# Latent-attention layer on one core: GpSimd forms the keys' rotary products from a copy made by ScalarE, zeros run on TensorE at the front, weight parts are shared out

## The reference, cut to what matters

```
xn  = layernorm(x)                                   # x [1, 2048, 512]
q   = xn @ wq                -> 16 heads of 128 + 64 (rotary part)
kva = xn @ wkv_a             -> ckv [2048, 128], k_pe [2048, 64]
ckv = ckv * rsqrt(mean(ckv^2) + eps) * kv_norm_scale
k_nope, v = ckv @ wkv_b      # per head 128 + 128
q_pe, k_pe = rope(q_pe), rope(k_pe)                  # k_pe is shared by all heads
attn = softmax(causal((q . k) * 192^-0.5)) ; out = (attn @ v) @ wo
x + out + (sum_r xn @ factors[r]) / sqrt(8) + bias
rope: [x1 * cos - x2 * sin, x2 * cos + x1 * sin]     # x1, x2: halves of 32
```

## Time and profile before

| | |
|---|---|
| median of 3 runs | 1505.07 us (1504.54 to 1505.99) |
| profiled execution, its own time | 1505.5 us |
| its span | 1503.7 us |
| busy: PE, DVE, ACT, POOL | 98%, 67%, 64%, 61% of the span |
| the span's first slice of 37.6 us | PE 50%, POOL 30% |
| first exponential of unit 0 starts | 61.43 us |

### The profile page before, as it was taken

The page is one execution under the profiler, slowest core; times in us unless marked ns, Lnnn a source line. Parts: engine busy times, 40 slices in busy tenths (PEclk is TensorE's granted clock), DMA queues, the critical chain, the costliest instruction groups (busy, mean ns, idle before and its releaser), DMA issues.

```text
span 1503.7 us, 25751 instructions
## 1 busy us (share of the span) xinstructions
PE 1471.3 (98%) x7908; PEld 755.5 (50%) x7908; DVE 1012.9 (67%) x2563; ACT 966.3 (64%) x2404; POOL 912.3 (61%) x919
## 2 busy tenths in 40 slices
PE   5999999999999999999999999999999999999997
PEld 5544555454545545445444444445555555455553
DVE  7877677777777766655555565566656666676776
ACT  7877767686866567566466666665546656654554
POOL 3688777675665456575465666656546555664553
PEclk9999999999999999999999999999999999999999
DMA  6599999987776597787577677886856677754554
GB/s 202 153 206 206 204 190 186 180 172 152 155 158 128 122 202 146 140 176 138 117 150 140 138 133 148 176 147 137 152 115 135 143 132 150 158 134 96 118 124 105
DMA packets 646615, 227.84 MB, mean 152 GB/s; under 512 B 599376, under 2 KB 612176, under 8 KB 646096
## 3 DMA queue, kind: packets, MB, share of 16 engines
q1 hardware_dynamic: 646480, 226.20, 73.6%
HBM read 65.67 MB, written 17.83 MB: 56 GB/s over the span
## 4 chain that ended last, share of the span: by engine, by line
PE 82%; ACT 6%; DVE 5%; issue 3%; POOL 3%; DMA 1%; SPq 0%; ACTq 0%; DVEq 0%; POOLq 0%
PE ps L423 17%; PE ps L424 16%; PE ps L425 16%; PE ps L574 6%; PE ps L579 6%; PE ps L580 6%; PE ps L576 6%; PE ps L575 6%; ACT ex L809 4%; POOL st L1400 2%; DVE gm L1166 1%; DVE ps L1168 1%; DMA acc<-x_in 0%; POOL q L1384 0%; ACT sqr L730 0%
## 5 line engine op out<-in xcount | busy, mean ns | idle before, releaser
L1400 POOL TENSOR_TENSOR st<-ex,st 128x512 f16<-128x512 f32 (+3 forms) x640 | 637.6, 1016 | 492.1 <-ACT st L819 482.2
L809 ACT ACTIVATE ex<-ps,nm,scales 128x512 f32<-128x512 f32 (+3 forms) x640 | 452.4, 709 | 459.0 <-DVE nm L1185 443.4
L1166 DVE TENSOR_REDUCE gm<-ps 128x1 f32<-128x512 f32 (+1 forms) x384 | 248.9, 668 | 168.8 <-PE ps L580 164.6
L819 ACT ACTIVATE st<-ex 128x512 f16<-128x512 f32 (+3 forms) x640 | 341.3, 561 | 6.1 <-ACT ex L809 0.4
L574 PE MATMUL ps<-kTh,q 128*128 128x512 f16 (+3 forms) x640 | 222.3, 347 | 6.8 <-ACT ex L809 4.5
L579 PE MATMUL ps<-kRh,q 128*128 128x512 f16 (+3 forms) x640 | 222.2, 347 | 2.5 <-POOL q L1384 2.5
L423 PE MATMUL ps<-pT,vH 128*128 128x512 f16 (+3 forms) x640 | 222.1, 347 | 0.6 <-DMA pT<-st 0.6
L580 PE MATMUL ps<-kRl,q 128*128 128x512 f16 (+3 forms) x640 | 222.1, 347 | 0.0
L575 PE MATMUL ps<-kTl,q 128*128 128x512 f16 (+3 forms) x640 | 222.1, 347 | 0.0
L576 PE MATMUL ps<-kTh,q 128*128 128x512 f16 (+3 forms) x640 | 222.1, 347 | 0.0
L424 PE MATMUL ps<-pT,vH 128*128 128x512 f16 (+3 forms) x640 | 222.1, 347 | 0.0
(11 more groups left out here) (202 smaller groups left out, 2141.3 us busy)
## 6 DMA issues: line engine op xcount, KB each, us to landing
wA<-w_abs SPq DMA_DIRECT2D x48, 256.0 KB, 2.9
wV<-w_vo SPq DMA_DIRECT2D x48, 256.0 KB, 2.9
pT<-st SPq DMA_TRANSPOSE x640, 3.3
fland<-factors_in SPq DMA_DIRECT2D x28, 256.0 KB, 3.0
wP<-w_pe SPq DMA_DIRECT2D x24, 256.0 KB, 3.0
wsq<-wq_in SPq DMA_DIRECT2D x16, 256.0 KB, 3.8
wso<-wo_in SPq DMA_DIRECT2D x16, 256.0 KB, 3.0
w_abs<-wA SPq DMA_DIRECT2D x16, 256.0 KB, 2.1
```

What stands on the lines that cost most here:

```text
L809: e.activation(ex[:, n % NEX, 0:keys], s_bank(n)[:, 0:keys], ACT.Exp, bias=nm[:, (i * QT + r) % 4:(i * QT + r) % 4 + 1], scale=scales[:, p ...
L819: e.activation(stage(n, keys)[:, :, 0, :], ex[:, n % NEX, 0:keys].rearrange("p (t n) -> p t n", n=P), ACT.Copy).then_inc(z["a_pH"], 1)
L1166: e.tensor_reduce(m, b, AX_X, ALU.max).then_inc(z["v_max"], 1)
L1400: e.tensor_tensor(s[:, :, 1, :], ex[:, n % NEX, 0:keys].rearrange("p (t n) -> p t n", n=P), s[:, :, 0, :], ALU.subtract).then_inc(z["g_pL" ...
```

## The change

1. The rotary products of the keys move from VectorE to GpSimd. GpSimd cannot take them from where TensorE left them, so ScalarE first copies the 64 raw numbers of both tiles into a new buffer `raw` (one instruction for a pair). VectorE keeps only the reciprocal, and its semaphore `v_kva` now stands for that.
2. The last tile (15) is normalized by GpSimd instead of ScalarE.
3. TensorE multiplies zeros (columns of the mask that are 0) before the first transposes (11 matmuls of 384 columns), before the norm of `wa` (5) and before the first latent product (7).
4. The low part of `wa` is halved: VectorE makes k blocks 0 and 1, GpSimd blocks 2 and 3 in two steps; TensorE waits for the second half between block 1 and block 2. VectorE makes it, and tile 1's low part, ahead of the statistics of pair 2; ScalarE makes tile 1's high part ahead of `wa`.
5. ScalarE makes the high parts of `wX` and `wA` for head 0, which VectorE made.
6. Squares of weights stand at other steps on ScalarE (`sq1` at step 1, `sqk` at 2, `sq0` at 3), and GpSimd normalizes tile 3 before it scales the key weights.
7. Two pairs of semaphores are merged (`v_rd` into `v_ts`, `d_bias2` into `d_bias`), which leaves the same instructions and the same waits.

```diff
-GTILES = tuple(range(3, 14, 2))
+GTILES = tuple(range(3, 16, 2))
...
@@ TensorE
+                    if t == 0 and k4 == KE // 2:
+                        e.wait_ge(z["g_wa"], 2)
...
+            def keep_busy(times):
+
+                for _ in range(times):
+                    e.matmul(s_bank(SBANKS - 1)[:, 0:CH - P], cmask[:, 0:P], cmask[:, 0:CH - P], start=True, stop=True)
+
             e.wait_ge(z["g_const"], 1)
+            keep_busy(11)
             for t in range(NT + 8):
                 if t < NT:
                     transpose_x(t)
                 if t == 1:
+                    keep_busy(5)
                     norm(("na", 0), ("a_sqa",), nra[:, :])
+                if t == 2:
+                    keep_busy(7)
...
@@ ScalarE
                 e.activation(ssq[:, 1, ts], ssq[:, 0, ts], ACT.Sqrt, bias=lat[:, 1:2],
                              scale=VS ** -2 / LORA).then_inc(z["a_rms"], 1)
+                if p2 >= 4:
+                    e.wait_ge(z["g_kk"], p2 - 3)
+                e.activation(raw[:, p2 % 4, :, :], b[:, :, LORA:QH], ACT.Copy).then_inc(z["a_raw"], 1)
...
+                if t == 11:
+
+                    e.wait_ge(z["v_w2"], 1)
+                    e.wait_ge(z["p_tq"], 1)
+                    e.activation(wX[:, 0, :], bank(("tq", 0)), ACT.Identity, bias=eps[:, 2:3],
+                                 scale=scales[:, 0, 0:1]).then_inc(z["a_hi"], 1)
+                if t == NT - 1:
+                    e.wait_ge(z["p_wabs"], 1)
+                    e.activation(wA[:, 0, 0, :], bank(("wabs", 0)), ACT.Copy, scale=1.0 / WS).then_inc(z["a_hi"], 1)
...
@@ VectorE
                 e.wait_ge(z["a_rms"], p2 + 1)
-                e.reciprocal(ssq[:, 2, ts], ssq[:, 1, ts]).then_inc(z["v_rr"], 1)
-                if p2 >= 4:
-                    e.wait_ge(z["p_kT"], p2 - 3)
-                e.tensor_tensor(turned[:, :, :, 0, :], halves, cos, ALU.mult)
-                for a in range(2):
-
-                    ins = e.tensor_tensor(ktmp[:, p2 % 4, :, a, :], halves[:, :, 1 - a, :], ropen[:, rows, 1 + a, :], ALU.mult)
-                ins.then_inc(z["v_kva"], 1)
+                e.reciprocal(ssq[:, 2, ts], ssq[:, 1, ts]).then_inc(z["v_kva"], 1)
...
+                    transpose_x(1)
+
+                    e.wait_ge(z["a_wa"], 1)
+                    e.scalar_tensor_tensor(out=wa[:, 1, 0:KE // 2, :], in0=wa_f[:, 0:KE // 2, :], scalar=lat[:, 0:1],
+                                           in1=wa[:, 0, 0:KE // 2, :], op0=ALU.mult, op1=ALU.subtract).then_inc(
+                                               z["v_wa"], 1)
...
@@ GpSimd
-                e.wait_ge(z["v_kva"], p2 + 1)
+                rows = both(p2)
+                halves = raw[:, p2 % 4, :, :].rearrange("p t (a n) -> p t a n", a=2)
+                if p2 == 0:
+                    e.wait_ge(z["d_ropen"], 16)
+                e.wait_ge(z["a_raw"], p2 + 1)
+                if p2 >= 4:
+                    e.wait_ge(z["p_kT"], p2 - 3)
+                e.tensor_tensor(turned[:, :, :, 0, :], halves,
+                                ropen[:, rows, 0, :].unsqueeze(2).broadcast_to([P, 2, 2, HALF]), ALU.mult)
+                for a in range(2):
+
+                    ins = e.tensor_tensor(ktmp[:, p2 % 4, :, a, :], halves[:, :, 1 - a, :], ropen[:, rows, 1 + a, :],
+                                          ALU.mult)
+                ins.then_inc(z["g_turn"], 1)
+                e.wait_ge(z["g_turn"], p2 + 1)
...
+            def latent_weights_low():
+
+                own = slice(KE // 2, KE)
+                scaled = rot[:, :, :].rearrange("p a n -> p (a n)")[:, 0:KE // 2 * QH].rearrange(
+                    "p (k n) -> p k n", n=QH)
+                e.wait_ge(z["v_lat"], 2)
+                e.tensor_scalar(scaled, wa_f[:, own, :], lat[:, 0:1], None, ALU.mult).then_inc(z["g_wa"], 1)
+                e.wait_ge(z["a_wa"], 1)
+                e.wait_ge(z["g_wa"], 1)
+                e.tensor_tensor(wa[:, 1, own, :], scaled, wa[:, 0, own, :], ALU.subtract).then_inc(z["g_wa"], 1)
```

More of the change, by code:

```diff
@@ L306, in build @@
             biasb = bias_sb[:, :]
+            raw = stage_one.enter_context(nc.sbuf_tensor("raw", [P, 4, 2, ROPE], F32))
             kt = [kt_sb[:, n, :, :] for n in range(4)]
@@ L333, in build @@
             "p_s", "p_pv", "p_na", "p_nf", "p_nrm", "p_nv",
[L335 removed]
+            "a_sqv", "a_sqo", "a_r4", "a_r8", "a_sqa", "a_sqp", "a_sq0", "a_sq1", "a_sqk", "a_sqf", "a_wa", "a_hi", "a_sd", "a_xn", "a_xt", "a_sq", "a_rms", "a_raw", "a_kk", "a_kT", "a_ff", "a_wpe", "a_wo",
             "a_q", "a_parts", "a_o", "a_exp", "a_pH",
[L338 removed]
+            "v_wa", "v_bn", "v_var", "v_rstd", "v_nmr", "v_xt", "v_kva",
             "v_kT", "v_ff", "v_scl", "v_na", "v_lat", "v_nf", "v_fstep", "v_fsc", "v_nrm",
[L340 removed]
+            "v_nv", "v_vroot", "v_vw", "v_vinv", "v_vsc", "v_w2",
             "v_fourth", "v_prod", "v_root", "v_inv", "v_tau", "v_scale", "v_tq_hi", "v_tq", "v_tkv_hi", "v_tkv", "v_wabs_hi", "v_wabs", "v_wvo_hi",
@@ L871, in _ @@
                     latent((t - 4) // 2)
-                if 1 <= t < NT:
+                if 2 <= t < NT:
                     transpose_x(t)
@@ L884, in _ @@
                     e.wait_ge(z["a_sqa"], 1)
+                    squares("sq1", 0)
+                if t == 2:
                     squares("sqk", 0)
-                if t == 2:
-                    squares("sq1", 0)
+                if t == 3:
+                    squares("sq0", 0)
                 if t == 5:
                     squares("sqp", 0)
-                if t == 6:
-                    squares("sq0", 0)
                 if t == 8:
                     w_pe(0)
+                if t == 11:
[6 more added lines that the diff above has]
+                    e.activation(wA[:, 0, 0, :], bank(("wabs", 0)), ACT.Copy, scale=1.0 / WS).then_inc(z["a_hi"], 1)
                 if t == NT + 1:
@@ L1044, in wq_transpose @@
                 size = scales[:, h // 2, 0:1]
-                e.tensor_scalar(wX[:, 0, :], b, size, None, ALU.mult).then_inc(z["v_tq_hi"], 1)
-                e.wait_ge(z["v_tq_hi"], h + 1)
+                if h:
+                    e.tensor_scalar(wX[:, 0, :], b, size, None, ALU.mult).then_inc(z["v_tq_hi"], 1)
+                    e.wait_ge(z["v_tq_hi"], h)
+                else:
+                    e.wait_ge(z["a_hi"], 1)
                 e.scalar_tensor_tensor(out=wX[:, 1, :], in0=b, scalar=size, in1=wX[:, 0, :], op0=ALU.mult,
@@ L1078, in w_abs @@
                     e.wait_ge(z[f"d_sA{h % 2}"], 16 * (h // 2))
-                e.tensor_scalar(wA[:, h % 2, 0, :], b, 1.0 / WS, None, ALU.mult).then_inc(z["v_wabs_hi"], 1)
-                e.wait_ge(z["v_wabs_hi"], h + 1)
+                if h:
+                    e.tensor_scalar(wA[:, h % 2, 0, :], b, 1.0 / WS, None, ALU.mult).then_inc(z["v_wabs_hi"], 1)
+                    e.wait_ge(z["v_wabs_hi"], h)
+                else:
+                    e.wait_ge(z["a_hi"], 2)
                 e.scalar_tensor_tensor(out=wA[:, h % 2, 1, :], in0=b, scalar=1.0 / WS, in1=wA[:, h % 2, 0, :],
@@ L1192, in denominators @@
                 e.tensor_reduce(tsum[:, i % 2, :], s, AX_X, ALU.add).then_inc(z["v_ts"], 1)
-                e.wait_ge(z["v_ts"], i + 1)
-                e.reciprocal(rtmp[:, i % 2, :], tsum[:, i % 2, :]).then_inc(z["v_rd"], 1)
-                e.wait_ge(z["v_rd"], i + 1)
+                e.wait_ge(z["v_ts"], 2 * i + 1)
+                e.reciprocal(rtmp[:, i % 2, :], tsum[:, i % 2, :]).then_inc(z["v_ts"], 1)
+                e.wait_ge(z["v_ts"], 2 * i + 2)
                 if i < H:
@@ L1275, in _ @@
                     norm_stats((t + 6) // 2)
-                if t == -2:
-                    e.wait_ge(z["a_wa"], 1)
-                    e.scalar_tensor_tensor(out=wa[:, 1, :, :], in0=wa_f, scalar=lat[:, 0:1], in1=wa[:, 0, :, :],
-                                           op0=ALU.mult, op1=ALU.subtract).then_inc(z["v_wa"], 1)
                 if t == 4:
@@ L1346, in add_bias @@
                 elif n == QT:
-                    e.wait_ge(z["d_bias2"], 16)
+                    e.wait_ge(z["d_bias"], 32)
                 if n >= 2 * QT and n % QT == 0:
@@ L1414, in _ @@
                             pattern=[[-1, CH]], channel_multiplier=1).then_inc(z["g_const"], 1)
+            normalize(3)
+            latent_weights_low()
             scale_keys(0)
-            normalize(3)
             normalize(5)
@@ L1671, in _ @@
                         e.wait_ge(z["v_wo"], H)
-                        load_bias(wso[:, :], "d_bias2")
+                        load_bias(wso[:, :], "d_bias")
                     if h == 1 and k >= 1:
```

12 lines of the change are left out of this document (3 added, 9 removed).

## The result

Measured: **1508.13 us** median of 14 runs (1505.17 to 1510.62) against 1505.13 of 14 runs of the kernel before (1504.12 to 1507.07). The ratio is 1.0016, 95% interval [1.0008, 1.0023]: slower by 0.16%. The forecast was 1505.2, so this is 2.9 us over it and 0.7 beyond the range's upper end. By the two measurements the loss is 1 to 3 us; the second, 1507.38, would lie at the range's upper end.

The account below looks back on a forecast made before the run. TensorE, busy 98% of the span, was taken as the bound, so only the front before the first exponential could give; the 0.5 us won there is used up by GpSimd, sum +0.1, forecast 1505.2 us by the median, range 1501.6 to 1507.4.

Parts of the forecast that it names:

- VectorE's new order: At 12 us: two things precede pair 2's statistics, so ScalarE's root comes at 15.2, 1.56 us later; ScalarE stands still from 13.0.
- ScalarE to 26 us: From the late root on, ScalarE reaches its next root at 26.36 against 25.85: half a microsecond lost, or 0.4.
- VectorE, 26 to 37 us: Two pairs' products leave VectorE, -0.9; starting 0.4 late, it lets tile 12's transpose come 0.5 earlier, at 36.7.
- High parts: VectorE's high parts of `wX` (0.73 us at 37.71) and `wA` (0.68 at 48.13) move to ScalarE: worth 0.
- GpSimd, 44 to 57 us: Three pairs get 1.0 us of products each; 1.58 us of idle time fills, and `keys(7)` starts at 56.7 against 56.62.
- the sum +0.1: Whole kernel: all parts together make it 0.1 us slower, 1505.6 by the profiled execution, 1505.2 by the median.
- Relief in full: Rival, in the front: everything VectorE loses counts, 5.5 us, giving 1499.6; chance 0.15.
- its own sign: What would show full relief of VectorE: no idle time on it up to 50 us and `keys(7)` at 54 or earlier.
- Half of it: Rival, in the front: late root costs less and 64-element products take 0.2; 2 to 3 us off, about 1502.6; chance 0.15.
- GpSimd blocked at the end: Rival, last three pairs: VectorE blocks GpSimd's products, 2.0 us per three instead of 1.0; +2.9 us, 1508.1; chance 0.10.
- Its other sign: For GpSimd's block at the front's end: it decides once a pair costs GpSimd more than 1.9 us in all.

Follow-up runs that it names:

- e9: The change itself, unaltered, measured again: 1507.38 us against 1506.24 of the kernel before, ratio 1.0007 [0.9998, 1.0016].
- e16: The kernel before with one GpSimd product (768 elements, some 1.9 us) put ahead of the last pair's sums: 1507.82 us, ratio 1.0016 [1.0007, 1.0024].
- e4: The change with all keys' rotary products back on VectorE and no raw copy on ScalarE: 1505.87 us, ratio 1.0004 [0.9996, 1.0013].
- e5: The change with 4 zero products ahead of the last keys' transposes and 9 behind them: 1506.30 us, ratio 1.0007 [0.9998, 1.0016].
- e6: The change with zero products ahead of tile 9's transpose (14), around the last keys' transposes (4, 9) and near 1485 us (13): 1506.43 us, ratio 1.0011.
- e7: The kernel before with the change's front zeros, plus 12 ahead of tile 9's transpose, 9 behind the last keys, 13 near the end: 1505.34 us, ratio 1.0001.

## Why the prediction was wrong, step by step

*VectorE's new order: right within the scatter of profiles.* The root that was forecast at 15.2 came at 14.60 in the first profile and at 15.30 in e9's; ScalarE stood still for it for 2.17 and 2.16 us, as foreseen. VectorE started its half of `wa` at 12.47 and 13.17, forecast 13.0. *ScalarE to 26 us:* 10.76 us from root to root in both profiles instead of 11.16, so the root forecast at 26.36 stood at 25.36 and 26.06. *VectorE, 26 to 37 us: an overestimate.* From that root to `rot` it took 18.48 us before and 18.07 in e9, so the relief was 0.41 where 1.0 had been forecast. At `rot` the two errors nearly cancel: 43.83 forecast, 43.99 and 44.13 measured. In the first profile this step took 18.63, for TensorE went through a fall of the clock between 31 and 35 us and ran its transpose of tile 12 at 37.05 without a wait; in e9, without that fall, the transpose waited 0.90 us for VectorE's low part and came at 37.17 (forecast 36.7):

```profile
37.17 0.66 PE L499 MATMUL ps<-ident,ex 128*128 128x128 f32 x4 [0.90 <-DVE kRl L1149]
```

*High parts:* nothing visible, as forecast.

*GpSimd, 44 to 57 us: the right mechanism, a term too small.* Forecast: `rot` at 43.83, a pair's three products 1.0 us, keys at 56.7, GpSimd without idle time, TensorE waiting for it. Measured: `rot` at 43.99, products and the wait behind them 1.09 a pair (54.97 to 56.06), keys at 57.07. From `rot` to the end of the last sums it took 12.93 us, with the 0.17 kept, against 12.77 forecast. So 0.16 came from the start, 0.16 from the products and 0.05 from the hand-over. Small as a term, but it stood against an edge: the sum +0.1 should have been +0.45, and set against the first scores it was 0.80. I had compared 56.7 with 56.62 and not asked what TensorE does meanwhile: 56.62 was no wait but the scores' end. GpSimd's sums had ended at 55.68 and the hand-over takes 0.15 (56.92 to 57.07), so 0.79 us of slack lay under it, and the change spent 1.59 (sums' end 1.32 us behind the first scores before, 2.91 after). Against VectorE's 0.45 a pair's 1.09 is 2.4 times. The Trainium skill, GPSIMD Engine Reference, Engine selection, has "~2× slower for 2-input ops", an estimated 0.9 a pair; the trace agrees in the direction, and the slowdown was more.

*The rivals.* Relief in full was wrong by its own sign: VectorE has idle time and no one behind it gains. Half of it was wrong too. "GpSimd blocked at the end" named the right place and 1508.1, within 0.1 of the result, for a reason the trace refutes, so that is luck: each of the last three pairs took 1.09, not 2.0. (Its other sign, a pair above 1.9 us in all, was met with 1.09 + 0.86, which the forecast's own 1.0 + 0.87 had all but reached.) A block there was once, elsewhere: two products of 64 elements took 1.05 us instead of 0.59 while VectorE's `wP` ran with two SBUF inputs.

```profile
33.90 1.05 POOL L1365 TENSOR_TENSOR ktmp<-raw,ropen 128x64 f32<-128x64 f32 x2
```

*The sum.* By the ledger: front up to the first query copy -0.34, A +0.82, B +0.71, C +0.34, or about +1.5 at the last unit's copy (1472.68 to 1474.19). The fall at 60 us adds 0.6 to 1.15 where it comes. D's two values, 1.7 apart, go with a fall of the clock near 1487 us (before: 0.77 in 1487 to 1492; in the change's profile 1.00), which nine of the 20 profiles have, with and without the change. The profile I had priced against contained it, the change's did not, which is why the two profiled times look alike while the medians do not. Of A's part e16 is the proof, and the table of the group; that C's 0.34 counts in the end time was not tried, and B's +0.71 is within its scatter.

## What to carry to other kernels

Before work is moved to an engine with idle time, find the last thing it delivers and how much slack its receiver has there: this GpSimd had 0.8 us in front of the last keys and was given three pairs of 1.09. An average of 61% says nothing about it. Moving six of eight pairs and keeping the last two cost nothing that could be measured; moving all eight cost 1 to 3 us.

When a step comes early and the end does not move, look for the next result that a queue issues in its own order: here a factor load stood behind five other DMAs, and nothing was left of a front that came 1.2 us earlier in e4's profile, and another order of two loads gave the kernel before a ratio of 0.9991 [0.9983, 1.0000].

And a pause of TensorE costs its length plus, in some executions, the slower products behind it. Compare several executions, with their clocks, before two profiles are set against each other, and measure the change twice: its ratio was 1.0016 and then 1.0007.

## What the runs showed of the hardware that I had not expected

- The granted clock goes back to 0.50 in a kernel that is 98% busy: behind 2.39 to 2.41 us of idle time (near 30 and 1485 us) and behind 0.73 (0.61 in e16) and 1.63 us (56 to 59), in some executions and not in others; behind the 1.63 without the 0.73 in none of ten profiles. In the change's profile it is 0.50 from 32 to 34 us.
- Zeros in the pauses keep it at 1.00 (e5, e6) but no gain in time is shown: e7 has the highest clock of its batch, 0.9994, and the time of the kernel before.
- VectorE pauses for 0.31 us for nothing that the profile shows, in the same place in all kernels with the last two pairs' products on GpSimd and in none of the others. It is C's 0.34. What it is was not tried:

```profile
609.35 0.75 DVE L1236 SCALAR_TENSOR_TENSOR acc<-ps,rden,acc 128x512 f32<-128x512 f32 x1 [0.31 <-issue]
```
